# A transformer layer on one core: an own set of banks for the fifth shared batch, and another order of the last sums

## The reference

```python
x = x + attention(layernorm(x), Wq, Wk, Wv, Wo, rel_emb)
...
xf = layernorm(x).reshape(-1, d)
sh = gelu(xf @ sw1 + sb1) @ sw2 + sb2                        # the shared expert, all 4096 tokens
logits = xf @ gate_w.T + expert_bias                        # 7 routed experts
topv, topi = top_k(logits, 2)
w = softmax(topv)
combine = sum(one_hot(topi, 7) * w[..., None], axis=1)
h = gelu(einsum('td,edh->eth', xf, rw1) + rb1[:, None, :])
out_e = einsum('eth,ehd->etd', h, rw2) + rb2[:, None, :]
x = x + sh + einsum('te,etd->td', combine, out_e)
```

## Time and profile before

| | us |
|---|---|
| median of 3 runs | 848.81 (846.87 to 850.23) |
| the profiled execution, its own time | 853.25 |
| its span | 851.4 |
| TensorE matmuls busy | 785.6 (92%) |
| VectorE busy | 620.7 (73%) |
| ScalarE busy | 477.5 (56%) |
| GpSimd busy | 252.5 (30%) |
| mean granted clock of TensorE | 0.943 |

### The profile page before, as it was taken

The page is one execution under the profiler, slowest core; times in us unless marked ns, Lnnn a source line. Parts: engine busy times, 40 slices in busy tenths (PEclk is TensorE's granted clock), DMA queues, the critical chain, the costliest instruction groups (busy, mean ns, idle before and its releaser), DMA issues. The chain is left out here.

```text
span 851.4 us, 18147 instructions
## 1 busy us (share of the span) xinstructions
PE 785.6 (92%) x6177; PEld 543.4 (64%) x6177; DVE 620.7 (73%) x1928; ACT 477.5 (56%) x720; POOL 252.5 (30%) x407
## 2 busy tenths in 40 slices
PE   4999889999999999999999997688878799999996
PEld 2777646666666666666656555455553499999954
DVE  5666588888888888888888832576765367667854
ACT  2444306666666666666666672465553177777720
POOL 1122011111121112111211110277776145655530
PEclk9999959999999999999999998699898689999998
DMA  4999894543564335443444813455513625556676
GB/s 118 279 350 355 281 221 106 161 116 94 131 167 133 95 106 169 131 117 114 125 138 135 278 61 126 153 185 181 165 71 101 189 84 150 168 158 206 199 259 235
DMA packets 74631, 140.75 MB, mean 165 GB/s; under 512 B 14520, under 2 KB 34640, under 8 KB 74366
## 3 DMA queue, kind: packets, MB, share of 16 engines
q1 hardware_dynamic: 62962, 116.91, 45.7%
q0 software_dynamic: 9792, 19.54, 7.0%
q10 hardware_dynamic: 1788, 3.18, 1.1%
HBM read 85.71 MB, written 56.78 MB: 167 GB/s over the span
## 5 line engine op out<-in xcount | busy, mean ns | idle before, releaser
L734 DVE CUSTOM_DVE_ANT_0 sums<-pS,near 128x512 bf16<-128x512 f32 x512 | 329.4, 687 | 47.7 <-PE pS L800 39.0
L767 ACT ACTIVATE prob<-pE 128x1024 f32<-128x1024 f32 x256 | 248.4, 1022 | 148.3 <-PE pE L825 148.3
L825 PEld LDWEIGHTS pE<-bandT,place 64*128 64x128 f32 x2048 | 166.1, 189 | 12.6
L825 PE MATMUL pE<-bandT,place 64*128 64x244 f32 (+2 forms) x2048 | 163.3, 271 | 0.0
L800 PE MATMUL pS<-k_st,q_st 48*128 48x512 f32 x512 | 138.3, 476 | 6.1 <-DMA k_st<-k_parts 3.5
L839 PE MATMUL pC<-prob,v_aug 128*32 128x512 f32 x1024 | 135.7, 604 | 1.0 <-ACT ctx_sb L775 1.0
L800 PEld LDWEIGHTS pS<-k_st,q_st 48*128 48x128 f32 x512 | 62.6, 192 | 115.2 <-DVE nmax L734 88.3
L817 PE MATMUL pE<-q_st,k_st 62*128 62x512 f32 x512 | 114.9, 406 | 2.0 <-issue 1.9
L1115 POOL DMA_INDIRECT expert_rows<-rb,xr x76 | 77.3, 1017 | 75.9 <-DVE rb L1328 61.3
L1099 POOL DMA_INDIRECT routed_rows<-xr,slot_i x64 | 65.2, 1019 | 33.4 <-issue 19.3
L1637 PE MATMUL pD<-w2p,hT 128*128 x456 | 63.8, 289 | 2.0 <-DVE hT L1321 1.6
(11 more groups left out here) (187 smaller groups left out, 1046.8 us busy)
## 6 DMA issues: line engine op xcount, KB each, us to landing
xr<-routed_rows SPq DMA_DIRECT2D x38, 258.0 KB
q_st<-q_parts SPq DMA_DIRECT2D x64, 128.0 KB, 2.7
k_st<-k_parts SPq DMA_DIRECT2D x64, 128.0 KB, 2.9
ctx<-ctx_sb SPq DMA_DIRECT2D x32, 256.0 KB, 2.8
q_parts<-qk SPq DMA_DIRECT2D x14, 512.0 KB, 8.2
k_parts<-qk SPq DMA_DIRECT2D x14, 512.0 KB, 7.6
near<-bias_by_distance SPq DMA_DIRECT2D x16, 448.0 KB, 5.0
xr<-expert_rows SPq DMA_DIRECT2D x14, 512.0 KB, 6.6
```

Source lines behind the costliest of these rows:

```text
L734: dve.tensor_tensor_reduce(sums[:, r % 4], pS[:, unit % PS], near[:, hg % 2, j, lead:lead + S], -1.0, BIG, ALU.add, ALU.min, nmax[:, j, t: ...
L767: act.activation(prob[:, par, 2 * step:2 * step + 2], pE[:, 2 * (step % 2):2 * (step % 2) + 2], ACT.Exp).then_inc(exp_done, 1)
L825: ins = pe.matmul(pE[:, bank + side, a:z], place[rows, half], bandT[rows, (quad // 2) % 2, pair, part, lead:lead + z - a], start=False, st ...
```

## The change

- Batch 4 (`IN_GAP`) gets banks of its own: its shares are turned into pX[:, 0, 1], its down products go to pX[:, 1], its hidden activations to `cn[:, 0]`, its shares to the part of hT that batch 6 has later. Its turn now stands between its two up halves.
- The up products and hidden activations of batch 5 move ahead of the tiles; the activations go to `cn[:, 1]`. Its down products stay behind the tiles.
- The waits for ScalarE and VectorE ahead of the first tile move to the first and second `expert_up`; ahead of batch 4's down products stand waits for the table to have read the counts from pX[:, 1, 0].
- Behind the tiles TensorE turns the shares of batches 5 and 6 first, then does the up products of 6, down of 5, up of 7, down of 6, turn and down of 7.
- VectorE adds the shared result of batch 5 after the second rows of batches 0 and 1, that of batch 6 after those of 2 to 5, and that of 7 last.

The diff:

```diff
@@ -49,6 +49,7 @@
 XW = D + 2
 EARLY = 3
 CB = 5
+IN_GAP = 4
 TILES_FROM = 5
 OWN = B - 2
 X2_SLOT = (0, 1, 0, 2, 1, 3, 0, 4)
@@ -944,16 +945,17 @@
             return pX[:, 1, m] if b == OWN else pU[:, m]
 
         def down_of(b, t2):
-            return pX[:, 0, t2].rearrange("p (u d) -> p u d", u=2) if b == OWN else pD[:, t2]
+            bank = pX[:, 0, t2] if b == OWN else pX[:, 1, t2] if b == IN_GAP else None
+            return pD[:, t2] if bank is None else bank.rearrange("p (u d) -> p u d", u=2)
 
         def hidden_of(b):
-            return cn[:, 0] if b == OWN else h_f
+            return cn[:, 0] if b in (IN_GAP, OWN) else cn[:, 1] if b == TILES_FROM else h_f
 
         def shares_of(b):
-            return hT[0:3 * NE, 0, 0] if b == OWN else cTs
-
-        def last_user(b):
-            return b - 2 if b > OWN else b - 1
+            return hT[0:3 * NE, 0, 0] if b in (IN_GAP, OWN) else cTs
+
+        def turned_shares_of(b):
+            return pX[0:3 * NE, 0, 1] if b in (IN_GAP, OWN) else pD[0:3 * NE, 1].rearrange("p u d -> p (u d)")
 
         def up_bank(i, m):
             return (pU[:, m] if i % 2 == 0 else pX[:, 1, m])[:, 0:TS]
@@ -1230,8 +1232,10 @@
 
                 def add(b):
                     xb = x1v(b)
-                    if b >= TILES_FROM:
-                        dve.wait_ge(s["y_acc"], b + 1)
+                    if b == B - 1:
+                        dve.wait_ge(s["y_acc"], B)
+                    elif b >= TILES_FROM:
+                        dve.wait_ge(s["yf_acc"], 2 * b + 2)
                     dve.wait_ge(s["xn2"], 4 * b + 4)
                     for t2 in range(2):
                         dve.wait_ge(s["d_mm"], 2 * b + t2 + 1)
@@ -1338,6 +1342,8 @@
 
                 def second_rows(b):
                     dve.wait_ge(s["yf_acc"], 2 * b + 2)
+                    if b == TILES_FROM or b == OWN:
+                        dve.wait_ge(s["sh_acc"], 2 * b + 2)
                     dve.wait_ge(yl_ld[b], 16)
                     dve.tensor_tensor(x1v(b), x1v(b), yl[b], ALU.add).then_inc(s["y_acc"], 1)
 
@@ -1391,8 +1397,11 @@
                     first_rows(k)
                 for b in range(B):
                     second_rows(b)
-                for b in range(TILES_FROM, B):
-                    add(b)
+                    if b == 1:
+                        add(TILES_FROM)
+                    elif b == OWN - 1:
+                        add(OWN)
+                add(B - 1)
 
             @block.scalar
             def _(act):
@@ -1432,17 +1441,24 @@
                     act.wait_ge(s["c_turn"], b + 1)
                     if b == OWN:
                         act.wait_ge(s["dn_mm"], NT)
-                    elif b >= 1:
-                        act.wait_ge(s["d_mm"], 2 * last_user(b) + 2)
-                    act.activation(shares_of(b), down_of(b, 1)[0:3 * NE].rearrange("p u d -> p (u d)"), ACT.Copy
-                                   ).then_inc(s["cT_done"], 1)
+                    elif b == B - 1:
+                        act.wait_ge(s["d_mm"], 2 * TILES_FROM + 2)
+                    elif b == TILES_FROM:
+                        act.wait_ge(s["d_mm"], 2 * EARLY + 2)
+                    elif 1 <= b <= EARLY:
+                        act.wait_ge(s["d_mm"], 2 * (b - 1) + 2)
+                    act.activation(shares_of(b), turned_shares_of(b), ACT.Copy).then_inc(s["cT_done"], 1)
 
                 def hidden(b, m):
                     act.wait_ge(s["u_mm"], 2 * b + m + 1)
-                    if b == TILES_FROM:
+                    if b == IN_GAP or b == TILES_FROM:
+                        act.wait_ge(s["wo_mm"], 2 * (B - 2 + b - IN_GAP) + 2)
+                    elif b == OWN:
+                        act.wait_ge(s["d_mm"], 2 * IN_GAP + 2)
+                    elif b == B - 1:
                         act.wait_ge(s["hlo"], NT)
-                    if b >= 1 and b != OWN:
-                        act.wait_ge(s["d_mm"], 2 * last_user(b) + 2)
+                    elif b >= 1:
+                        act.wait_ge(s["d_mm"], 2 * (b - 1) + 2)
                     act.activation(hidden_of(b)[:, m], up_of(b, m), ACT.Gelu, bias=b1s[:, NE - 1, m:m + 1]).then_inc(s["h_done"], 1)
 
                 def x_high(i):
@@ -1493,10 +1509,11 @@
                             weights_hi(k)
                     if i + 1 < B:
                         normalise(i + 1, 1)
-                for b in range(EARLY + 1, TILES_FROM):
-                    hidden(b, 0)
-                    hidden(b, 1)
-                    shares(b)
+                hidden(IN_GAP, 0)
+                shares(IN_GAP)
+                hidden(IN_GAP, 1)
+                hidden(TILES_FROM, 0)
+                hidden(TILES_FROM, 1)
                 act.wait_ge(s["tab_done"], 2)
                 experts = ()
                 for k in range(-3, NT):
@@ -1507,12 +1524,11 @@
                         weights_copy(k + 3, experts[k + 3])
                     if 0 <= k + 2 < NT:
                         gelu(k + 2, experts[k + 2])
-                for b in range(TILES_FROM, B):
+                shares(TILES_FROM)
+                shares(OWN)
+                for b in (OWN, B - 1):
                     hidden(b, 0)
                     hidden(b, 1)
-                    if b == OWN:
-                        shares(OWN - 1)
-                        shares(OWN)
                 shares(B - 1)
 
             @block.tensor
@@ -1569,22 +1585,25 @@
 
                 def turn_shares(b):
                     pe.wait_ge(s["comb_done"], 3 * b + 3)
-                    if b == TILES_FROM:
+                    if b == IN_GAP:
+                        pe.wait_ge(s["lg_done"], B)
+                    elif b == TILES_FROM:
                         pe.wait_ge(s["ev_done"], 2 * NT)
-                    if b == OWN:
+                    elif b == OWN:
                         pe.wait_ge(s["xlo"], NT)
+                    elif b == B - 1:
+                        pe.wait_ge(s["sh_acc"], 2 * TILES_FROM + 2)
                     elif b >= 1:
-                        pe.wait_ge(s["sh_acc"], 2 * last_user(b) + 2)
-                    flat = down_of(b, 1)[0:3 * NE].rearrange("p u d -> p (u d)")
+                        pe.wait_ge(s["sh_acc"], 2 * (b - 1) + 2)
                     for t in range(TT):
-                        ins = pe.transpose(flat[:, P * t:P * t + P], raw(combine_p[:, b % CB, t]), ident[:])
+                        ins = pe.transpose(turned_shares_of(b)[:, P * t:P * t + P], raw(combine_p[:, b % CB, t]), ident[:])
                     ins.then_inc(s["c_turn"], 1)
 
                 def shared_up(b, m):
-                    if b == TILES_FROM:
+                    if b >= OWN:
                         pe.wait_ge(s["hhi"], 2 * NT)
-                    if b >= 1 and b != OWN:
-                        pe.wait_ge(s["h_done"], 2 * last_user(b) + m + 1)
+                    elif b >= 1:
+                        pe.wait_ge(s["h_done"], 2 * (b - 1) + m + 1)
                     for c in range(MC):
                         ins = pe.matmul(up_of(b, m), w_sh[:, 0, c, P * m:P * m + P], x2T(b)[:, c],
                                         start=c == 0, stop=c == MC - 1)
@@ -1594,8 +1613,11 @@
                     pe.wait_ge(s["b2_split"], 2)
                     pe.wait_ge(s["h_done"], 2 * b + 2)
                     pe.wait_ge(s["cT_done"], b + 1)
-                    if b >= 1 and b != OWN:
-                        pe.wait_ge(s["sh_acc"], 2 * last_user(b) + 2)
+                    if b == IN_GAP:
+                        pe.wait_ge(s["pads_done"], 1)
+                        pe.wait_ge(s["tab_chain"], 3 * B + 2)
+                    elif 1 <= b <= EARLY:
+                        pe.wait_ge(s["sh_acc"], 2 * (b - 1) + 2)
                     for t2 in halves:
                         for u in range(2):
                             t = 2 * t2 + u
@@ -1619,6 +1641,10 @@
                     pe.wait_ge(s["xlo"], i + 1)
                     pe.wait_ge(s["wc_hi"], i + 1)
                     pe.wait_ge(s["wc_lo"], i + 1)
+                    if i == 0:
+                        pe.wait_ge(s["h_done"], 2 * TILES_FROM + 2)
+                    elif i == 1:
+                        pe.wait_ge(s["sh_acc"], 2 * TILES_FROM)
                     if i >= 2:
                         pe.wait_ge(s["hhi"], 2 * (i - 1))
                     for m in range(2):
@@ -1669,17 +1695,17 @@
                     if i % 2 == 0 and i >= 2:
                         shared_down(i // 2 - 1, (1,))
                 turn_shares(EARLY)
-                shared_up(EARLY + 1, 0)
+                shared_up(IN_GAP, 0)
                 pe.wait_ge(s["tab_chain"], 3 * B)
                 pe.matmul(pX[:, 1, 0, 0:2 * NE], ones_b[:], cum[:, B], start=True, stop=True).then_inc(s["cnt_mm"], 1)
-                shared_up(EARLY + 1, 1)
+                turn_shares(IN_GAP)
+                shared_up(IN_GAP, 1)
                 shared_down(EARLY)
-                turn_shares(EARLY + 1)
```

(15 more changed lines are left out.)

## The result

The changed kernel takes 840.89 us in the median of 12 runs (835.27 to 845.24); before takes 846.06 in the median of its 12 (840.16 to 850.54). The ratio is 0.9925, 95% interval 0.990 to 0.995: 4.2 to 8.5 us less, 6.3 in the middle (the two medians differ by 5.2). The forecast was 8.8 less and 840.0, in a range of 834.5 to 845.5; the time lies in the range and the gain is clear of noise. That 840.0 is met to 1 us is luck: before's median came down from 848.8 in 3 runs to 846.1 in 12, the gain came out smaller than forecast, and the two nearly cancel. The change was run once more beside the experiments, on another chip: 0.9949 (0.991 to 0.9988).

What follows compares the result with a forecast made beforehand. It took TensorE's waits on both sides of the tiles, over shared bank pD, and the low clock after them as the bound. 3.25 ahead + 7.5 behind - 2.0 clock = 8.8 us; 848.8 - 8.8 = 840.0, range 834.5 to 845.5.

Steps and rivals of the forecast that it cites:

- The mechanism ahead of the tiles: Ahead of the tiles: batch 4's own banks remove TensorE's waits; work ends at 672.4, then the first tile's load decides.
- the 3.25 us: Ahead of the tiles: the tiles start at 675.3 instead of 678.55, 3.25 us earlier, bounds 2 to 3.75.
- the gain is in places that every execution has: Whole kernel: the 8.8 us taken from the profiled execution was subtracted in full from the runs' median of 848.8.
- The clause in brackets: Whole kernel: part of the 4.4 us between profiled execution and median may be clock luck in the stretches repaired.
- Behind the tiles the order: Behind the tiles: after a new 2.1 us wait, TensorE ends at 840.4 against 848.27, VectorE's sums fitting into gaps.
- The transfers' term: At the end: transfers still running as the last store begins take 0.4 us (0 to 1.3) off, leaving 7.5.
- a sign of being wrong: At the end: transfers full when the last half is stored was listed among observations that would show the prediction wrong.
- The clock's fall behind the tiles (2.0 us): Behind the tiles: the new 2.1 us wait more likely than not lowers TensorE's clock, costing 2.0 us.
- rival B: No clock fall behind the tiles, perhaps a shorter low stretch at their start: 10.75 to 12.5 less, 836.3 to 838.0; chance 0.28.
- D: Behind the tiles: the low clock lasts some 18 us, costing 9; 1.8 us less, 847, counted as same; chance 0.07.
- E: Behind the tiles: the low clock holds through the tail, 25.8 us of work taking 51.6; slower, 864; chance 0.03.
- C: Tiles start at most about 1 us earlier, by an early clock fall or late first load: 6.6 less, 842.2; chance 0.12.

Runs made afterwards that it cites:

- the new sums alone: Kernel before the change with only VectorE's new order of second rows and shared sums; TensorE's and ScalarE's lists unchanged: 836.14 us, ratio 0.9940.
- the old sums: Changed kernel with VectorE's earlier order put back, all second rows first, then the shared sums of batches 5, 6 and 7: 837.96 us, ratio 0.9948.
- before with few stores: Kernel before the change without the output stores of batches 0 to 3 (2.1 MB of 4.2): ratio 1.0015.
- before with two and one spare matmuls: Kernel before the change with unused matmuls added, two ahead of the turn of batch 7 and one before its down products: ratio 1.0002.
- The run with the up products first: Changed kernel with batch 6's up products moved ahead of the turns of batches 5 and 6 behind the tiles: 834.16 us, ratio 0.9920.
- the changed kernel with few stores: Changed kernel without the output stores of batches 0 to 3 (2.1 MB of 4.2): ratio 0.9929.
- The two parts alone: Changed kernel with VectorE's earlier order of sums, ratio 0.9948, and kernel before the change with only VectorE's new order of sums, ratio 0.9940.
- up products first, few stores: Changed kernel with batch 6's up products ahead of the turns behind the tiles, and without the output stores of batches 0 to 3: ratio 0.9903.

## Why the prediction came out as it did

- **The mechanism ahead of the tiles was right**, and its steps too: the turn right behind the count, no wait, 5.6 us for the down products, the end of the work at 671.15, 16.8 us after the count, where I had 17.0. The first load was issued at 16.8 (17.1 in the earlier trace rows) and landed 2.8 us later, as estimated. The tiles started 3.6 us sooner between the two profiles, against 3.25.
- **Its size was wrong for the median.** I carried the 3.25 us over to every execution ("the gain is in places that every execution has"). That sentence is the step that failed: the profile of before took 853.25 us, more than any of its 12 runs. What the new order can gain at the start is how much later than the first load's landing the old order begins the tiles. The load landed 2.65 to 2.80 us after its issue in the eight profiles in which TensorE waited for it; with 2.7 us for the others, an estimate, the five profiles of the old order give 3.4 (before), 3.2, 1.8, 1.3 and, with the new sums alone, 0 us: 1.9 on average. In the first four the down products of batch 4 ran at the low level, in the last they did not. The clause in brackets, that clock luck might be part of the 4.4 us, named the cause and gave it no size.
- **The same holds behind the tiles.** The wait for batch 5's sum is not in every execution of the old order of sums: 2.44 us in before's profile and 3.21 in that of the old sums, but none in before with few stores and in before with two and one spare matmuls. In these two the first load of second rows went 6.2 to 6.3 us after the last tile (7.7 in before's profile), and the up products of batch 5 ran at the low level at first. Their stretches are 34.5 us and, with 2.6 us of spare work in it, 36.1, against 39.0 in before's profile and 32.6 in the changed kernel's.
- **Behind the tiles the order was right**: a wait of 2.17 us (2.1 forecast), sums in VectorE's gaps, no wait before the turn of batch 7, TensorE done 27.8 us after the last tile (28.0).
- **The transfers' term was too small**: 0.4 us forecast, 1.7 measured (4.06 against 2.40 us from the last sum to the end). The transfers were full when the last half was stored (DMA share 1.01 to 1.03 from 830 to 836 us), which the prediction had named as a sign of being wrong. The run with the up products first shows more of it: TensorE 1.8 us sooner, nothing gained.
- **The clock's fall behind the tiles (2.0 us) did not come** in the changed kernel's two profiles, after waits of 2.17 and 2.83 us; it came after 2.96 in the changed kernel with few stores, where it cost 1.4 us. So a short fall was a fair guess for a part of the executions, and in its profile the change went the way of rival B, with 10.0 us in the two stretches against its 10.75. In the median a baseline that is often better than its profile and the transfers took more than the clock gave back: 6.3 us against 8.8, which is outside the interval's 8.5 by little.
- D and E are out. C, 842.2 and 6.6 us less, was a better guess of the gain than of the reason: the start gains less than 3.25 us on average since before's own start is often not so late.
- **Open**: the stretches of these profiles speak for some 8 us or more, the first ratio for 4 to 8.5. That before's profile is its longest execution goes some way to explain it, but one or two profiles of a kernel are too few to say how far. The two parts alone, 0.9948 and 0.9940, add to more than the whole; with intervals of 3 us either side that tells nothing of how they add.

## What to carry over

An engine that works its list in order should have each sum in it at the place where its inputs are due, not grouped by kind: a few lines that put two shared sums between loads gave 5.5 of the 6.4 us behind the tiles, between single profiles. Before a stall is priced from one profile, look how long that execution was among its runs: a low clock in the very stretch makes the repair look larger than it is. And when TensorE's wait goes, read what the next thing to be late already costs in the executions that had luck: here a DMA that stood behind seven small stores and behind the scattered rows, and 8.4 MB of transfers at the end.

## What the runs showed of the hardware

- The length of TensorE's wait doesn't decide alone whether the granted clock falls, or when. Behind 2.17 and 2.83 us (the changed kernel, behind the tiles) it did not fall. Behind 2.77 us (the changed kernel, ahead of the tiles), 2.96 and 3.23 us (few stores) the next group ran at the low level. Behind 1.91, 2.53 (new sums), 3.03 (up products first, few stores, ahead of the tiles) and 3.21 us (old sums) the next group still ran at the high level, and the clock fell 1.2 to 1.4 us after its start. The Trainium skill (TensorE: Matmul & The Clock Gate, "HAM oscillation — how this bites in real kernels") tells of a kernel in which each wait for a load throttles the clock, so that the next group starts cold; of these nine waits, three went that way.
- The same seven pad stores took SP 9.1 to 9.3 us on one chip and 11.5 to 12.0 on others, and the stretch of tiles 127.8 to 129.1 us on that one and in the last group, 131.6 to 134.1 in the others.
- ScalarE and VectorE have short waits that the profile puts down to no engine of the kernel ("remote"): 0.75 to 2.3 us at ScalarE's first instructions behind the tiles in four profiles, and 0.8 to 1.8 us ahead of VectorE's last evictions in three profiles of the changed order. What they are is not shown here.
